# Graph network: fade factors in SBUF, and three steps of the attention stage on GpSimd

## The reference, cut to what matters

```
attn = sum(Q[dst] * K[src]) * scale + edge_bias[edge_type]     # 8 heads
mx = segment_max(attn, dst);  ex = exp(attn - mx[dst])
sm = segment_sum(ex, dst);    a = ex / (sm[dst] + 1e-16)
out = segment_sum(a * V[src], dst) @ Wo + bo
x = layernorm(x + out, g1, be1)
x = layernorm(x + gelu(x @ W1 + b1) @ W2 + b2, g2, be2)
...
x = layernorm(x_in + that)          # the layer's own outer norm, no gain
```

## Time and profile before

| | us |
|---|---|
| median of 3 runs | 3549.31 (3548.37 to 3552.37) |
| span of the profiled execution | 3856.9 |
| attention stage, first to last `gap` (49 groups) | 2574.8 to 3197.2 |
| VectorE busy, 2650 to 3150 | 482.36 of 500 |
| ScalarE busy, 2650 to 3150 | 476.85 of 500 |
| TensorE busy, 2650 to 3150 | 460.35 of 500 |
| GpSimd busy, 2650 to 3150 | 347.20 of 500 |

### The profile page before, as it was taken

One profiled execution on the slowest core, in us unless ns is written; L12 is line 12 of the kernel. 1 busy time (PEld: TensorE's weight loads), 2 busy tenths in 40 slices (PEclk: granted clock), 3 DMA queues, 4 the chain that ended last, 5 costly groups with the idle time before them and its releaser, 6 DMA issues. The chain is left out here.

```text
span 3856.9 us, 54369 instructions
## 1 busy us (share of the span) xinstructions
PE 3033.4 (79%) x11490; PEld 2023.8 (52%) x11490; DVE 2725.5 (71%) x6900; ACT 2299.0 (60%) x5259; POOL 2523.9 (65%) x2721
## 2 busy tenths in 40 slices
PE   3124149999999998899979999979999996777676
PEld 2012035555555555777759999955555553343333
DVE  3005749999999998777769989969999994222222
ACT  2003039999999999777623333439999994232332
POOL 5750069999999998777534444436666763666665
PEclk7557569999999999899989999989999997777777
DMA  5012025555555554444323343322322321222221
GB/s 190 1 36 90 1 76 171 171 168 169 171 164 175 164 176 141 113 123 119 109 86 112 114 112 110 109 81 72 88 83 84 86 82 44 72 73 72 72 68 46
DMA packets 262118, 404.65 MB, mean 105 GB/s; under 512 B 61938, under 2 KB 104135, under 8 KB 262033
## 3 DMA queue, kind: packets, MB, share of 16 engines
q1 hardware_dynamic: 204920, 304.18, 24.6%
q0 software_dynamic: 44032, 73.90, 8.4%
q10 hardware_dynamic: 13081, 25.69, 2.0%
HBM read 213.15 MB, written 194.37 MB: 106 GB/s over the span
## 5 line engine op out<-in xcount | busy, mean ns | idle before, releaser
L256 POOL TENSOR_TENSOR dn_rstd<-dn_var,w_minus_half 128x4 f32<-128x4 f32 x294 | 292.6, 1002 | 16.7 <-DVE dn_var L241 16.5
L1603 POOL DMA_INDIRECT m_src<-table_x,e_src_first x196 | 191.1, 975 | 127.5 <-issue 52.1
L1603 POOL DMA_INDIRECT p_src<-table_x,e_src x196 | 213.1, 1087 | 93.0 <-issue 53.6
L2491 POOL DMA_INDIRECT out_rows<-m_x,e_out_first x196 | 197.6, 1008 | 94.0 <-issue 65.8
L648 POOL DMA_INDIRECT scratch_node_row<-o_own,e_out x196 | 192.0, 979 | 90.7 <-issue 62.4
L1643 POOL DMA_INDIRECT g_own<-in_x,e_dst x196 | 223.9, 1142 | 36.9 <-issue 36.9
L2576 DVE TENSOR_TENSOR m_y<-m_bout,m_own 128x512 f32<-128x512 f32 x49 | 33.9, 692 | 294.3 <-DMA a_typ<-in_type_row 166.3
L1603 POOL DMA_INDIRECT a_src<-table_x,e_src x196 | 200.9, 1025 | 47.6 <-issue 37.5
L1634 POOL DMA_INDIRECT g_src<-scratch_wide,e_src x196 | 192.0, 980 | 58.8 <-issue 46.0
L1409 PE MATMUL n_banks<-w_gru_both,d_xT 128*128 128x256 f32 x784 | 223.6, 430 | 8.6 <-ACT d_xT L1446 8.6
L1409 PEld LDWEIGHTS n_banks<-w_gru_both,d_xT 128*128 128x128 f32 x784 | 192.9, 327 | 71.3 <-ACT d_xT L1446 68.6
(11 more groups left out here) (486 smaller groups left out, 9952.8 us busy)
## 6 DMA issues: line engine op xcount, KB each, us to landing
table_x<-d_x SPq DMA_DIRECT2D x294, 256.0 KB, 2.0
g_src<-in_x_wide SPq DMA_DIRECT2D x97, 262.0 KB
scratch_wide<-g_src SPq DMA_DIRECT2D x97, 262.0 KB
out_rows<-d_x SPq DMA_DIRECT2D x97, 256.0 KB
s_x<-in_x ACTq DMA_DIRECT2D x31, 768.0 KB
table_x<-d_xT SPq DMA_DIRECT2D x49, 256.0 KB
scratch_post<-d_x SPq DMA_DIRECT2D x49, 256.0 KB, 2.0
p_rc<-scratch_rcount SPq DMA_DIRECT2D x49, 256.0 KB
```

The lines of the kernel that those rows point to most:

```text
L256: pool.tensor_tensor(self.rstd[s][:], self.var[s][:], minus_half[:], ALU.pow).then_inc(self.rooted[s], 1)
L1603: pool.indirect_dma_start(out=self.rows[s][:, t * P:(t + 1) * P], out_offset=None, in_=self.table, in_offset=bass.IndirectOffsetOnAxis(ap= ...
L2491: pool.indirect_dma_start(out=D["out"], out_offset=bass.IndirectOffsetOnAxis(ap=Ed.out_first[:, at:at + 1], axis=0), in_=x4[s][:, t * P:(t ...
```

## The change

Five things change in `attention_edges` and in its last norm; the list `AT` does not.

1. BELOW and EXP_FADE write a new SBUF tile `fade` (one for each slot) instead of the PSUM bank, and the two scans read it from there. The bank, now `bank_fit`, holds only the logits.
2. LOGITS on TensorE therefore waits for the other slot's DIFFER only, no longer for its two scans. BELOW gets a wait for the slot's previous SUM_VALUES.
3. ABOVE moves from ScalarE to GpSimd, as a maximum with 0.
4. BIAS_OWN moves from ScalarE to GpSimd.
5. The addition of epsilon to the last variance moves from VectorE's MOMENTS to GpSimd, in front of LAST_ROOT, in the new functions `begin_moments` and `root_of_moments`.

```diff
+    def begin_moments(self, dve, i, s, y):
+        for t in range(TPG):
+            dve.bn_stats(self.st[s][:, t, :], y[:, t * P:(t + 1) * P]).then_inc(self.stats_made[s], 1)
+        wait(dve, self.stats_made[s], i * 2 * TPG + TPG)
+        self.mem.settle(dve)
+        for t in range(TPG):
+            dve.bn_aggr(self.mv[s][:, t, :], self.st[s][:, t, :]).then_inc(self.stats_made[s], 1)
+
+    def root_of_moments(self, pool, i, s, minus_half):
+        wait(pool, self.stats_made[s], i * 2 * TPG + 2 * TPG)
+        pool.tensor_scalar(self.var[s][:], self.mv[s][:, :, 1], EPS, None, ALU.add).then_inc(self.summed[s], 1)
+        self.root(pool, i, s, 0, minus_half)
...
                 if k == LAST_ROOT:
-                    last.root(pool, i, s, 0, W.minus_half)
+                    last.root_of_moments(pool, i, s, W.minus_half)
+                if k == ABOVE:
+                    wait(pool, differed[s], i + 1)
+                    wait(pool, prob_summed[s], i)
+                    wait(pool, weighed[s], i)
+                    pool.tensor_scalar(prob[s][:], gap[s][:], 0.0, None, ALU.max).then_inc(split[s], 1)
+                if k == BIAS_OWN:
+                    wait(pool, own_spread[s], i + 1)
+                    wait(pool, x_turned[s], i)
+                    pool.tensor_scalar(x2bT[s][:], ownT[s][:], W.c_be2[:, 0:1], None, ALU.add).then_inc(biased[s], 1)
...
                 if k == LOGITS:
                     wait(pe, hot_made[s], i + 1)
                     wait(pe, matched[s], i + 1)
-                    wait(pe, prob_summed[s - 1], before(i, s))
-                    wait(pe, values_summed[s - 1], before(i, s))
+                    wait(pe, differed[s - 1], before(i, s))
...
-                if k == ABOVE:
-                    wait(act, differed[s], i + 1)
-                    wait(act, prob_summed[s], i)
-                    wait(act, weighed[s], i)
-                    act.activation(prob[s][:], gap[s][:], ACT.Relu).then_inc(split[s], 1)
                 if k == BELOW:
                     wait(act, differed[s], i + 1)
-                    act.activation(bank_fade[:], gap[s][:], ACT.Relu, scale=-1.0).then_inc(split[s], 1)
+                    wait(act, values_summed[s], i)
+                    act.activation(fade[s][:], gap[s][:], ACT.Relu, scale=-1.0).then_inc(split[s], 1)
...
-                    act.activation(bank_fade[:], bank_fade[:], ACT.Exp, scale=-1.0).then_inc(exped[s], 1)
+                    act.activation(fade[s][:], fade[s][:], ACT.Exp, scale=-1.0).then_inc(exped[s], 1)
...
-                    dve.tensor_tensor_scan(backward(den[s]), backward(bank_fade), backward(prob[s]), den[s - 1][:, 0:1],
+                    dve.tensor_tensor_scan(backward(den[s]), backward(fade[s]), backward(prob[s]), den[s - 1][:, 0:1],
                                            ALU.mult, ALU.add).then_inc(prob_summed[s], 1)
...
-                    dve.tensor_tensor_scan(backward(acc[s]), backward(bank_fade), backward(pv[s]), acc[s - 1][:, 0:1],
+                    dve.tensor_tensor_scan(backward(acc[s]), backward(fade[s]), backward(pv[s]), acc[s - 1][:, 0:1],
                                            ALU.mult, ALU.add).then_inc(values_summed[s], 1)
...
                 if k == MOMENTS:
                     wait(dve, joined[s], i + 1)
-                    last.moments(dve, i, s, y3[s])
+                    last.begin_moments(dve, i, s, y3[s])
```

More of the change, by code:

```diff
@@ L2116, in attention_edges @@
     yT, n, nT, h, n2, x2bT, y3, x3, broad = (rows(name) for name in ("yT", "n", "nT", "h", "n2", "x2bT", "y3", "x3", "broad"))
+    fade = rows("fade")
     peak, inv = rows("peak", GROUP + 1), rows("inv", TPG * HEADS)
@@ L2120, in attention_edges @@
     hot = [mem.sb(f"a_hot{s}", [3 * TYPES, GROUP], BF16) for s in range(S)]
-    bank_src, bank_own, bank_v, bank_fade, bank_y, bank_x = (mem.ps("a_b" + n) for n in ("src", "own", "v", "fade", "y", "x"))
+    bank_src, bank_own, bank_v, bank_fit, bank_y, bank_x = (mem.ps("a_b" + n) for n in ("src", "own", "v", "fit", "y", "x"))
     bank_ff = [mem.ps(f"a_bff{s}") for s in range(S)]
@@ L2236, in step @@
                     wait(pe, matched[s], i + 1)
-                    wait(pe, prob_summed[s - 1], before(i, s))
-                    wait(pe, values_summed[s - 1], before(i, s))
-                    pe.matmul(bank_fade[:], W.head_bias[:], hot[s][:], start=True, stop=False)
-                    pe.matmul(bank_fade[:], W.heads[:], qk[s][:], start=False, stop=True).then_inc(logits[s], 1)
+                    wait(pe, differed[s - 1], before(i, s))
+                    pe.matmul(bank_fit[:], W.head_bias[:], hot[s][:], start=True, stop=False)
+                    pe.matmul(bank_fit[:], W.heads[:], qk[s][:], start=False, stop=True).then_inc(logits[s], 1)
                 if k == TURN_SUM:
@@ L2310, in step @@
                     outer.scale_by_scalar(act, i, s, 0, n[s], bank_y)
[L2311 to L2314, removed]
                 if k == N_COPY:
@@ L2362, in step @@
                     wait(dve, differed[s], i)
-                    dve.tensor_tensor_scan(backward(peak[s][:, 0:GROUP]), backward(bank_fade), backward(low[s]), peak[s - 1][:, 0:1],
+                    dve.tensor_tensor_scan(backward(peak[s][:, 0:GROUP]), backward(bank_fit), backward(low[s]), peak[s - 1][:, 0:1],
                                            ALU.max, ALU.add).then_inc(peaked[s], 1)
@@ L2368, in step @@
                     wait(dve, split[s], 2 * i)
-                    dve.tensor_tensor(gap[s][:], peak[s][:, 1:], bank_fade[:], ALU.subtract).then_inc(differed[s], 1)
+                    dve.tensor_tensor(gap[s][:], peak[s][:, 1:], bank_fit[:], ALU.subtract).then_inc(differed[s], 1)
                 if k == WEIGH:
```

## The result

The changed kernel takes 3704.74 us (3699.88 to 3705.95, four runs) against 3550.26 for the kernel before in the same comparison: a ratio of 1.0432, with a 95% interval of 1.0418 to 1.0447. It is slower by 154 us. The forecast was slower by 96, with a range that ended at 3680.

What follows compares the result with a forecast made beforehand. VectorE was taken to set the attention stage's period; -0.08 (al_var) - 0.11 (a_keep) + (1.1 - 0.11) + 1.34 = +2.14 us, times 45 periods, is +96 us on 3549: 3645 us, range 3583 to 3680.

Steps and rivals of the forecast that it cites:

- both waits: VectorE waiting for GpSimd at SHIFT and at FF_SCALE in each attention period; 65% for both as worked out, 3645 us.
- The second: At FF_SCALE: scans with two SBUF inputs hold GpSimd's an_rstd and the fetch behind it; VectorE waits 1.34 us a period.
- the first: At SHIFT: ABOVE ahead of HOT, al_var and LAST_ROOT on GpSimd delays al_rstd; VectorE waits 1.1 - 0.11 us a period.
- The 0.11: VectorE's wait for the load of a_keep, 0.11 us a period, was to vanish because the load gets time.
- only the first wait: Rival: the scan lets GpSimd's root pass, so FF_SCALE does not wait; +36 us, 3585 us, chance 15%.
- the other way round: Rival: a GpSimd root also holds VectorE's SUM_VALUES, 0.41 us more a period; 3663 us, chance 7%.
- a, the length of ABOVE: Duration of ABOVE on GpSimd, taken as 1.1 us, between 0.63 and 1.59.
- The stage ran at full clock, so I carry the sum over unscaled: Attention's granted clock was 1.00, so +96 us was added whole, giving 3645 us; scaled by 0.92, 3637.
- no third wait: After FF_SCALE everything in the period is late by the same 1.34 us, so VectorE waits nowhere else.
- This shortens nothing: ScalarE losing ABOVE and BIAS_OWN, 1.37 us a period, gains nothing because ScalarE already waits for VectorE.
- Faster: ScalarE set the pace: Rival: ScalarE feeds VectorE late, so relieving it gains 9 us if GpSimd is on time; 3540 us, chance 5%.
- none of them waited: Between two peaks, 12.93 us, VectorE's rows carry no bracket, read as VectorE never waiting and setting the period.

Runs made afterwards that it cites:

- e1_fade: The kernel before with only the fade factors moved from PSUM to SBUF, the three moves to GpSimd left out: 3617.99 us, ratio 1.0181.
- c_before: The kernel before, unchanged, run once more for a profile whose span is that of the timed runs: 3552.25 us.
- e3_above: The kernel before with ABOVE alone moved to GpSimd: 3614.27 us, ratio 1.0171.
- e2_psum: The changed kernel with the fade factors back in PSUM, the three moves to GpSimd kept: 3653.27 us, ratio 1.0283.
- e10_three: The kernel before with all three moves to GpSimd, fade factors in PSUM, HOT and the loads moved in the table AT: 3579.77 us, ratio 1.0071.
- e4_fill: The changed kernel with two more unread products of 512 columns on TensorE in each period: 3676.69 us, ratio 1.0353.
- e5_psum_fill: The changed kernel with fade factors back in PSUM and two more unread products on TensorE in each period: 3609.10 us, ratio 1.0151.
- e8_early: The kernel before with the epsilon addition on GpSimd and HOT and the loads moved in the table AT: 3551.56 us, ratio 0.9992.
- e9_early_above: The kernel before with the epsilon addition and ABOVE on GpSimd, and HOT and the loads moved in AT: 3539.79 us, ratio 0.9959.

## Why the prediction was wrong, step by step

**Right: both waits, their places and their mechanisms.** The second was forecast at 1.34 us and is 1.30; the first was forecast at 0.99 and is 1.25, for the reason in the next paragraph. an_rstd was to last 2.0 and lasts 1.94, the fetch behind it 1.4 and lasts 1.56. e1_fade shows it alone: 63 us with little of the clock in it (granted 0.98), where the step gave 45 x (1.34 - 0.11) = 55. The 0.11 is part of the difference: it was to come back when the load of a_keep had time, the wait for it is nearly gone in e1_fade (0.5 us in 500), but the period is not shorter by it (14.34 = 12.94 + 1.40). The rival "only the first wait" has fallen, and so has "the other way round": a_acc starts at 2705.36 inside the held root and takes its 1.28.

**The term that was mis-sized: a, the length of ABOVE.** "One input should cost somewhat less than two, so a = 1.1." It took 1.51, more than the two-input sum of the same shape (1.29), and BIAS_OWN 1.59. The nearer row was HOT, the same instruction with other types, at 1.59. That is 45 x 0.41 = 18 us. The Trainium skill's loop of 769 ns (GPSIMD Engine Reference, Elementwise, side-by-side cycle accounting) was further off; the measurement decides.

**The step that failed: TensorE's clock, put at nothing.** "The stage ran at full clock, so I carry the sum over unscaled", and "Late next: everything behind FF_SCALE by the same amount, so no third wait." Both assume that TensorE keeps 2.4 GHz when its pauses grow. It did not: the new waits leave it idle for some 3 us in one piece in each period, its granted clock falls to 0.91 on the mean, and in the slow stretches its products arrive late for the peak and for DIVIDE (a_o). By the median this pause is 0.5 us in c_before (clock 1.00), 1.4 in e1_fade (0.98), 2.0 in e3_above (0.95), 2.1 in e2_psum (0.90) and 3.0 in the change (0.91); in e10_three it is 0.9, and the clock 1.00. e4_fill gives back 28 us of that by adding work, e5_psum_fill 44 us. Of the 58 us by which the forecast fell short, some 7 lie outside the stage and are no more than profiles differ by there. Of the 51 in the stage (147 - 96), 18 are a by the formula, 23 are the clock's as far as e4_fill gives them back, and some 10 stay open. Two places for them can be estimated from the periods. Those of e4_fill, with its clock of 0.98, are 15.77 us on the mean and 15.66 where undisturbed, 45 x 0.11 = 5 us; and the 0.11 for a_keep could not come back in full, since the mean period of c_before is only 0.03 over the 12.94 of its undisturbed ones, 45 x 0.08 = 4 us. Neither was tried by itself, and al_var, below, goes the other way.

**ScalarE's relief: right for this kernel, wrong in reason.** "This shortens nothing": true beside the two waits. But I took ScalarE's waits for the gap as proof that it had time to spare, and e8_early and e9_early_above show that it set the pace in another part of the same period (an_sq), together with VectorE. The rival "Faster: ScalarE set the pace" has this right, though it could not show behind the two waits; and "none of them waited", read from rows without a bracket, could not have seen it. Likewise al_var was put at 0.08 us; with its wait for al_mv it costs VectorE 0.2 (the starts of al_mv and a_yT are 0.49 to 0.50 apart before and 0.29 to 0.30 after).

## What to carry to other kernels

When a step moves to an engine with spare time, add it to that engine's queue and look at who waits behind it: the share of busy time says nothing about it. With HOT out of its way the same move of ABOVE turned 60 us of loss into 15 us of gain; the other changes of that version gave 3.6 us by themselves (e8_early), which cannot be told from none. Before an operand moves from PSUM to SBUF, look for instructions of VectorE that then read two SBUF tensors, and for GpSimd's work beside them. Look also for an engine that is ready at almost the same moment as the one that sets the pace: relieving one of the two gave nothing here, relieving both did. A wait that leaves TensorE idle can cost twice, once by itself and once by the clock; if the sum opens a pause of some us on TensorE in a stage at full clock, give that a term.

## What the runs showed of the hardware

- A scan of VectorE with both inputs in SBUF holds a GpSimd root that starts inside it: 1.945 us instead of 1.042, the median of 49 in e1_fade. In the row shown of the change it ends 0.83 us behind the scan. A fetch by an indirect DMA is held as well, 1.56 instead of 1.02, and ends 0.82 behind it. The scan that starts inside the held root keeps its 1.28.
- A 128x512 f32 pass of GpSimd with one input takes 1.51 (maximum with a constant) and 1.59 us (sum with a column), more than the 1.29 of the sum of two tensors.
- A short VectorE instruction that starts inside a 128x512 pass of GpSimd ends with that pass, although the next GpSimd instruction follows at once (al_var in e3_above, 0.47 instead of 0.17 us); the VectorE instruction behind it started 0.08 us after it all the same.
- Two products more in each period on TensorE, read by nobody, made a kernel 44 us faster (3653.27 to 3609.10), with the granted clock of the stage going from 0.90 to 1.00. The logits' two products took 1.12 us at a clock of 1.00 and 2.08 in a stretch at 0.57.
